# Two head groups of attention outputs brought to token rows in one set of products, and divided in one pass

## The reference

```python
x = L0_attn_x                                     # (16, 512, 128)
q = (x @ Wq.T + bq).reshape(B, T, H, hd).transpose(0, 2, 1, 3)   # H = 16, hd = 8; k and v alike
zq, zk, zv = q @ V, k @ V, v @ V                  # rank 8
att = softmax(einsum('bhqr,bhkr->bhqk', zq, zk) / sqrt(rank))
y_r = einsum('bhqk,bhkr->bhqr', att, zv)
y = (y_r @ U.T).transpose(0, 2, 1, 3).reshape(B, T, D)
x = layernorm(x + y @ Wo.T + bo)
# then the experts, and a second layernorm
```

## Time and profile before

| | |
|---|---|
| Median of 3 runs | 1186.22 us (1182.94 to 1187.09) |
| The profiled execution | 1182.22 us |
| Its span, first to last instruction | 1180.3 us |
| TensorE busy | 1044.4 us (88%) |
| VectorE busy | 971.2 us (82%) |
| ScalarE busy | 901.0 us (76%) |
| GpSimd busy | 588.4 us (50%) |
| Time between the same instruction of two neighbouring batches | 47.86 us |
| Mean granted TensorE clock, share of full speed | 0.972 |

### The profile page before, as it was taken

One profiled execution on the slowest core, in us unless ns is written; L12 is line 12 of the kernel. 1 busy time (PEld: TensorE's weight loads), 2 busy tenths in 40 slices (PEclk: granted clock), 3 DMA queues, 4 the chain that ended last, 5 costly groups with the idle time before them and its releaser, 6 DMA issues. The chain is left out here.

```text
span 1180.3 us, 24741 instructions
## 1 busy us (share of the span) xinstructions
PE 1044.4 (88%) x7711; PEld 512.6 (43%) x7711; DVE 971.2 (82%) x2117; ACT 901.0 (76%) x1161; POOL 588.4 (50%) x823
## 2 busy tenths in 40 slices
PE   4589999999999999999999999897459999999967
PEld 2232223232232222222323222222249999999952
DVE  4688898989989999899899998991458888888845
ACT  1177888788788887887878878778259999999827
POOL 1124318256273472643825627314347777777745
PEclk9899999999999999999999999999669999999989
DMA  2832242232322413324234232200022222222246
GB/s 72 262 100 74 63 118 72 84 106 71 109 70 82 136 47 107 91 64 130 74 83 115 65 98 71 79 14 19 21 72 70 67 71 68 70 69 69 64 181 255
DMA packets 105461, 104.88 MB, mean 89 GB/s; under 512 B 21608, under 2 KB 82834, under 8 KB 105376
## 3 DMA queue, kind: packets, MB, share of 16 engines
q1 hardware_dynamic: 94912, 81.88, 24.6%
q0 software_dynamic: 8448, 16.93, 4.5%
q10 hardware_dynamic: 2016, 4.98, 1.1%
HBM read 56.06 MB, written 47.39 MB: 88 GB/s over the span
## 5 line engine op out<-in xcount | busy, mean ns | idle before, releaser
L802 DVE TENSOR_REDUCE row_max<-score_ps 128x2 f32<-128x1024 f32 x512 | 618.4, 1220 | 71.8 <-PE score_ps L573 68.7
L688 ACT ACTIVATE probs<-score_ps 128x1024 f32<-128x1024 f32 x512 | 522.0, 1023 | 115.6 <-PE score_ps L555 93.6
L849 POOL DMA_INDIRECT routed_d<-rows,slot_i x128 | 126.7, 990 | 316.6 <-DVE slot_i L771 270.2
L536 PE MATMUL av_ps<-probs,v_one 128*9 128x512 f32 x2048 | 267.7, 595 | 6.8 <-ACT probs L688 5.9
L573 PE MATMUL score_ps<-k_stack,q_stack 48*128 48x512 bf16 x1024 | 199.6, 387 | 49.9 <-ACT probs L688 26.3
L555 PE MATMUL score_ps<-q_stack,k_stack 51*128 51x512 bf16 x1024 | 199.1, 386 | 18.3 <-DVE row_max L802 13.7
L1110 ACT ACTIVATE w_cur<-experts 128x1156 f32 x136 | 158.5, 1167 | 36.6 <-PEq L415 17.2
L555 PEld LDWEIGHTS score_ps<-q_stack,k_stack 51*128 51x128 bf16 x1024 | 48.9, 92 | 298.4 <-issue 166.2
L1206 POOL DMA_INDIRECT y_d<-y_out,place x136 | 137.0, 1007 | 44.5 <-issue 44.5
L1067 PE MATMUL up_ps<-xt_sb,w_cur 128*128 128x128 f32 x1088 | 146.2, 278 | 0.5 <-DVE xt_sb L1143 0.4
L1075 PE MATMUL down_ps<-w_cur,hidden_r 128*128 128x128 f32 x1088 | 143.4, 275 | 0.0
(11 more groups left out here) (186 smaller groups left out, 1110.6 us busy)
## 6 DMA issues: line engine op xcount, KB each, us to landing
k_stack<-k_stack_d SPq DMA_DIRECT2D x128, 96.0 KB, 2.5
q_stack<-q_stack_d SPq DMA_DIRECT2D x128, 96.0 KB, 2.5
x_rows_sb<-routed_d SPq DMA_DIRECT2D x136, 65.0 KB
q_stack_d<-q_parts SPq DMA_DIRECT2D x32, 192.0 KB
k_stack_d<-k_parts SPq DMA_DIRECT2D x30, 192.0 KB
x_in<-L_attn_x SPq DMA_DIRECT2D x16, 256.0 KB, 3.7
q_stack_d<-q_parts SPq DMA_DIRECT2D x32, 128.0 KB
x_res<-L_attn_x SPq DMA_DIRECT2D x16, 256.0 KB, 3.5
```

Of the source, the lines that this page charges most:

```text
L536: last = nc.tensor.matmul(av_ps[32 * g:32 * g + V_COLS, :], v_one[n.parity][:, kb, HG * hg + g, :], probs[:, (2 * j + g // 2) % P_RING, g ...
L688: nc.scalar.activation(probs[:, s % P_RING, :, :], exp_bank(b, s)[:, :, :], ACT.Exp).then_inc(S["exp_done"], 1)
L802: nc.vector.tensor_reduce(row_max[:, m // (STEPS // 2), :, m % (STEPS // 2)], max_bank(b, s)[:, :, :], AX.X, ALU.max).then_inc(S["red_done ...
L849: nc.gpsimd.indirect_dma_start(routed_d, bass.IndirectOffsetOnAxis(ap=slot_i[n.parity][:, w, t:t + 1], axis=0), rows[n.parity][:, w, t, :] ...
```

## The change

Where `y_transpose` ran four times a batch (steps 17, 21, 29, and 3 of the next batch) with four transposes each, a function `y_rows` runs twice (step 21, and step 3 of the next batch) for two head groups. It doesn't transpose: for each of the four token tiles and each of the two groups it multiplies the piece of `y_sb` (the stationary operand) with the 36 columns of the identity that hold values, 4 times 9. So it is 8 ordinary float32 products of 36 columns, where two `y_transpose` were 8 transposes of 128 columns. The results of both groups lie side by side in `misc_ps`, and `y_normalise` divides them together, at steps 22 and 4: a reciprocal of 32 sums a token instead of 16, and a multiplication over 8 heads instead of 4. The steps 17 and 29 have no use of `misc_ps` any more.

```diff
-                            if s == 3 and prev:
-                                y_transpose(p1, 3)
+                                y_rows(p1, 1)
...
-                            if s == 17 and cur:
-                                emptied(s)
-                                y_transpose(b, 0)
...
                             if s == 21 and cur:
                                 emptied(s)
-                                y_transpose(b, 1)
+                                y_rows(b, 0)
...
-                            if s == 29 and cur:
-                                emptied(s)
-                                y_transpose(b, 2)
...
-                        def y_transpose(n, hg):
-                            pe.wait_ge(S["y_ready"], n.count(HG, hg + 1))
+                        def y_rows(n, two):
+                            pe.wait_ge(S["y_ready"], n.count(HG, 2 * two + 2))
+                            used = ident[:, :].rearrange("p (g c) -> p g c", c=P // HG)[:, :, 0:V_COLS]
+                            width = HG * V_COLS
                             for t in range(QT):
-                                last = nc.tensor.transpose(misc_ps[:, t * P:(t + 1) * P], y_sb[hg % 2][:, t * P:(t + 1) * P], ident[:, :])
+                                for k in range(2):
+                                    at = (2 * t + k) * width
+                                    last = nc.tensor.matmul(misc_ps[:, at:at + width], y_sb[k][:, t * P:(t + 1) * P], used, start=True, stop=True)
                             last.then_inc(S["yt_done"], 1)
...
-                            wait(act, S["yt_done"], n.count(HG, hg - 1))
+                            wait(act, S["yt_done"], n.count(2, hg // 2))
...
-                        def y_normalise(n, hg):
-                            dve.wait_ge(S["yt_done"], n.count(HG, hg + 1))
-                            ps = misc_ps[:, :].rearrange("p (t g c) -> p t g c", t=QT, g=HG)
-                            nc.vector.reciprocal(inv_sum[:, hg, :, :], ps[:, :, :, R]).then_inc(S["yn_inv"], 1)
-                            dve.wait_ge(S["yn_inv"], n.count(HG, hg + 1))
+                        def y_normalise(n, two):
+                            heads = H // 2
+                            dve.wait_ge(S["yt_done"], n.count(2, two + 1))
+                            ps = misc_ps[:, 0:QT * heads * V_COLS].rearrange("p (t h c) -> p t h c", t=QT, h=heads)
+                            nc.vector.reciprocal(inv_sum[:, two, :, :], ps[:, :, :, R]).then_inc(S["yn_inv"], 1)
+                            dve.wait_ge(S["yn_inv"], n.count(2, two + 1))
                             wait(dve, S["ynt_done"], n.count(1, 0))
-                            nc.vector.tensor_tensor(y_norm[:, :, HG * hg:HG * hg + HG, :], ps[:, :, :, 0:R],
-                                                    inv_sum[:, hg, :, :].unsqueeze(3).to_broadcast([P, QT, HG, R]), ALU.mult).then_inc(S["yn_sb"], 1)
+                            nc.vector.tensor_tensor(y_norm[:, :, two * heads:(two + 1) * heads, :], ps[:, :, :, 0:R],
+                                                    inv_sum[:, two, :, :].unsqueeze(3).to_broadcast([P, QT, heads, R]), ALU.mult).then_inc(S["yn_sb"], 1)
...
-                            if s == 18 and cur:
+                            if s == 22 and cur:
                                 y_normalise(b, 0)
-                            if s == 22 and cur:
-                                y_normalise(b, 1)
-                            if s == 30 and cur:
-                                y_normalise(b, 2)
```

More of the change, by code:

```diff
@@ L147, in build_layer @@
             y_sb = [asb(f"y_sb{n}", [P, T]) for n in range(2)]
-            inv_sum = asb("inv_sum", [P, HG, QT, HG])
+            inv_sum = asb("inv_sum", [P, 2, QT, H // 2])
             y_norm = asb("y_norm", [P, QT, H, R])
@@ L421, in emptied @@
                         def emptied(s):
-                            order = ((1, proj, "xt_sb", n2, 1, 1), (3, prev, "yn_sb", p1, HG, 4), (5, prev2, "slot_step", p2, SLOT_STEPS, 2),
+                            order = ((1, proj, "xt_sb", n2, 1, 1), (3, prev, "yn_sb", p1, 2, 2), (5, prev2, "slot_step", p2, SLOT_STEPS, 2),
                                      (7, prev, "ynt_sb", p1, 1, 1), (9, cur, "negmax_sb", b, 2, 2), (11, prev, "res_ready", p1, 1, 1),
-                                     (13, proj, "q_sb", n2, 1, 1), (15, proj, "k_sb", n2, 1, 1), (17, cur, "yn_sb", b, HG, 1),
-                                     (19, nxt, "v_sb", n1, 1, 1), (21, cur, "yn_sb", b, HG, 2), (23, prev, "x1t_sb", p1, 1, 1),
-                                     (25, nxt, "negmax_sb", n1, 2, 1), (27, prev, "logits_sb", p1, 1, 1), (29, cur, "yn_sb", b, HG, 3))
+                                     (13, proj, "q_sb", n2, 1, 1), (15, proj, "k_sb", n2, 1, 1),
+                                     (19, nxt, "v_sb", n1, 1, 1), (21, cur, "yn_sb", b, 2, 1), (23, prev, "x1t_sb", p1, 1, 1),
+                                     (25, nxt, "negmax_sb", n1, 2, 1), (27, prev, "logits_sb", p1, 1, 1))
                             earlier = [e for e in order if e[0] < s and e[1]]
@@ L431, in emptied @@
                                 pe.wait_ge(S[name], n.count(per_batch, events))
-                            elif prev:
-                                pe.wait_ge(S["yn_sb"], p1.count(HG, 3))
                             elif prev2:
@@ L456, in misc @@
                             if s == 7 and prev:
-                                pe.wait_ge(S["yn_sb"], p1.count(HG, 4))
+                                pe.wait_ge(S["yn_sb"], p1.count(2, 2))
                                 emptied(s)
@@ L785, in body @@
                             if s == 4 and prev:
-                                y_normalise(p1, 3)
+                                y_normalise(p1, 1)
                             if s == 12 and prev:
                                 layernorm(p1)
-                            if s == 18 and cur:
+                            if s == 22 and cur:
                                 y_normalise(b, 0)
-                            if s == 22 and cur:
-                                y_normalise(b, 1)
-                            if s == 30 and cur:
-                                y_normalise(b, 2)
                             if s == 13 and prev:
```

## The result

The changed kernel is slower: 1216.9 us in the median (1213.3 to 1218.25), against 1184.58 for the kernel before (1182.78 to 1187.09) in the same comparison. The ratio is 1.0282, 95% interval 1.0262 to 1.0302. The forecast was 1211, range 1198 to 1223. The profiled execution took 1215.74 us with a span of 1213.8, that is 33.5 us more than the span before. One execution of all that follow, 1522.57 us in e10_v_at_17_gate_at_29 at a mean granted clock of 0.646, was in a slower state and counts in no ratio.

The account below looks back on a forecast made before the run. A ring of TensorE and ScalarE was taken as the bound. 1.02 + 0.68 us a batch over fifteen batches is 25.5, plus 2.3 for the last: 27.8 us on 1182.2, 1210, taken as 1211; range 1198 to 1223.

Parts of the forecast that it names:

- The bound: TensorE and ScalarE wait for each other in a ring; a delay of TensorE comes back through ScalarE undiminished.
- Price of the products: y_rows on TensorE: 16 weight loads at 0.11 us, 1.88 us in place of 0.59, 1.29 more at each place.
- Case (b): Rival: VectorE holds the batch, from step 29 to step 4, and its savings give 1175 us, faster; chance 0.05.
- the two bounds of the sum: Totals if y_rows took 1.49 us (about 14 us slower, 1197) or 2.18 us (about 36 us slower, 1219).
- Step 21: First joint place: 1.29 us more, 0.27 of it slack, so maxima of step 22 comes 1.02 us later each batch.
- Step 3: Second joint place: TensorE goes on 0.68 us later at step 6, where scores had waited 0.44 for a row maximum.
- case (c): Rival: slack at steps 22 and 6 is gone after the shift, 40 us, 1226; 0.14 together with dearer products.
- The division: VectorE, steps 22 and 4: 0.64 us for two groups instead of 0.49 for one, beside TensorE's scores and maxima.
- The end of the stage: Last batch: its step 21 about 0.9 us, its step 3 1.29 + 0.15 us; 2.3 us together.
- What is taken away: Transposes at steps 17 and 29 (0.59 us) and division at 18 and 30 (0.49 us): removing them gives nothing.
- Case (a): Rival: TensorE's 1.40 us more work a batch fits into its waits and is absorbed; no change, 1186 us; chance 0.10.

Follow-up runs that it names:

- e10_v_at_17_gate_at_29: e2_transposes with the product for v moved from step 19 to 17 and the gate's logits from 27 to 29; 1192.1 us, ratio 1.0068.
- e12_step21_only: Kernel before, with head groups 0 and 1 joined at step 21 by y_rows, groups 2 and 3 left as before; 1202.73 us, ratio 1.016.
- e1_unread: Changed kernel with four transposes that nobody reads put back at each of steps 17 and 29; 1213.32 us, ratio 1.0263.
- e5_before_late_copy: Kernel before, with the copy of av_ps on ScalarE placed behind its step's exponential instead of ahead; 1185.5 us, ratio 1.0026.
- e2_transposes: Changed kernel with 8 transposes, using an identity with reordered columns, in place of the 8 products at each joint place; 1189.59 us, ratio 1.005.
- e8_divided_twice: Changed kernel with each reciprocal and each multiplication of the joint division done twice; 1225.9 us, ratio 1.0357.

## Why the prediction was right

**The bound.** Right: a ring of TensorE and ScalarE in which a burst's excess is passed on undiminished, beyond the slack at its place. e12_step21_only shows it for one place (1.05 of 1.32 us), e1_unread shows that idle TensorE time elsewhere is worth nothing. The copy of `av_ps` is a link of it, as the prediction had it, though with 0.19 us of its 0.60 (e5_before_late_copy).

**Price of the products.** 1.88 us forecast, 1.90 and 1.91 measured; the pitch of 0.11 us and the 16 loads stand in the trace, and 8, 36 and 128 columns come out nearly alike. The excess is 1.32 instead of 1.29. TensorE's work was to grow by 1.40 us a batch; its busy time grew by 0.92. That difference is open, but busy time isn't a clean measure here: in e2_transposes it fell by 0.86 us (44.30), though the distance from each burst to the next `scores` says 0.32. That nothing but its stationary columns counts for a load, as the prediction says, isn't so in this kernel: the bf16 loads of the ranks come at 0.02 us with the same 128 columns. The float32 loads that the sum uses did come at 0.11.

**Case (b)** was tied to a `y_rows` of less than 1.06 us, since both bursts would then fit into the slack of 0.27 and 0.68 us. That is wrong twice. The slack at step 3 was put at 0.17 + 0.44 = 0.61 us by the prediction's own rows; 0.68 was what is left of 1.29 behind it. And one place can't use the slack of the other. e2_transposes took 1.02 us a place and was still 0.24 a batch slower. The same slip stands in the two bounds of the sum, 1197 and 1219 us, which take off 0.95 where 0.27 + 0.61 is 0.88: they are some 1 us too low each. The forecast itself took off the right sum.

**Step 21.** 1.02 us forecast, 1.06 in the timeline, 1.05 in its own experiment.

**Step 3** is the term that was mis-sized: 0.68 forecast, 0.95 in the timeline, 0.97 in its own experiment. The prediction asked at step 6 only what `scores` had waited for, and found 0.44 us of slack behind VectorE; that slack was there and was used (`scores` came 0.64 us later, and waits for nothing). But `maxima` is the next link, and it needs the exponential of step 5. Before, that ended at 412.20 us and `maxima` started at 412.45, so it had only some 0.2 us of slack, and no row ahead of the forecast shows it as a wait, since `maxima` was held by `scores` ahead of it. The exponential came 1.14 us later, and 1.32 - 0.17 - 0.20 = 0.95. This is case (c) in part: the exponential came later as the products did.

**The division** was priced at 0.64 us for both groups and took 0.74; the reciprocal over 32 sums lasts 358 ns, not the 0.27 us assumed. It changed nothing, since it lay beside TensorE's products: e8_divided_twice put 0.8 us more on VectorE at each place and 0.24 a batch came through. VectorE's row maximum of step 22 came 452.39 - 449.64 = 2.75 us after the burst instead of 1.74, 1.01 later, 0.9 forecast. The forecast that VectorE would be busy for 43.2 us was wrong by the busy time (44.09), which rose by 0.17. The records of neighbours overlap (two row maxima in succession count 2.35, a lone one 1.22), so a queue with more waits counts as busier, and a saving of 0.7 can't be read from that total.

**The end of the stage** was priced at 2.3 us (the last step 21 and the last step 3) and cost 5.3, of which the slower clock in the last `y_rows` alone is 3.60 - 1.97 = 1.6 (the `av` ahead of it took 1.74 us instead of 1.05); the second stage gave 1.5 back, for a reason that stays open. The sum of 27.8 us was 5.7 short of the 33.5: 29.75 - 25.5 = 4.2 in the fifteen batches, step 3 with 15 x 0.27 = 4.1, and 5.3 - 2.3 - 1.5 = 1.5 in the end of the stage and behind it.

**What is taken away** gave nothing, as forecast. Case (a) falls with the 1.99 us a batch, though TensorE is idle for 3.77 us in each: the question is not whether the added work fits into an engine's idle time but whether it fits into the slack of the place where it stands.

## What to carry to other kernels

Count weight loads, not columns, as long as the columns are few: in these traces a float32 product with a 128-column stationary operand costs two loads, a float32 transpose one, and shrinking the moving side from 128 to 36 columns saved 0.07 us of 1.09. Where engines hold each other in a ring, work joined into one burst uses the slack of one place instead of two; price it place by place, and look for slack that isn't drawn as a wait because another link was later by a hair. Following only the wait that is shown misses the next constraint behind it.

## What the runs showed of the hardware

The reciprocal on VectorE has a steep price per element: 128x16 from PSUM takes 248 ns in the mean, 128x32 takes 358, 6.9 ns for each further element a row, where the multiplication goes from 291 to 424 ns for 128 more, 1.0 ns each.

The thin end of the first stage doesn't run at one clock. The changed kernel and e1_unread have the same batch, but the last `y_rows` took 3.60 us in the one and 1.95 in the other, at a granted clock of 0.55 and 0.65 between 860 and 880 us:

```profile
860.00:880.00 20.00, 9.85 (x57) 6.80 (x54) 4.22 (x19) 4.57 (x9) 5.01 (x8) 0.55 0.03 11
```

```profile
860.00:880.00 20.00, 9.04 (x64) 6.28 (x59) 4.22 (x19) 5.23 (x10) 6.67 (x10) 0.65 0.04 14
```

The spans were 1213.8 and 1211.1 us, although the second kernel does more work. So 3 us of a whole time here, and some 6 in e8_divided_twice, can come from there; the length of a batch is the cleaner measure. It is not shown what decides the clock in that stretch: e1_unread has its unread transposes there too (64 matmul records instead of 57), but no run varied that alone.
